# Softmax-weighted sums issued two key tiles at a time, with a third buffer of exponentials

## What is computed

```python
def _spatial_experts(xn, idx, in_w, in_b, out_w, out_b):      # S
    qkv = jnp.einsum('btd,bed->bte', xn, in_w[idx]) + in_b[idx][:, None, :]
    ...
    att = jax.nn.softmax(jnp.einsum('bthd,bshd->bhts', q, k), axis=-1)
    o = jnp.einsum('bhts,bshd->bthd', att, v).reshape(B, T, D)
...
    logits = jnp.where(causal, logits, -jnp.inf)               # T
    att = jax.nn.softmax(logits, axis=-1)
    o = jnp.einsum('bhts,bshd->bthd', att, v).reshape(B, T, D)
```

## Time and profile before

| | us |
|---|---|
| three runs, median (lowest to highest) | 1758.8 (1756.96 to 1760.89) |
| the profiled execution, its own time | 1757.12 |
| its span, first to last instruction | 1755.3 |
| TensorE busy | 1584.6 |
| VectorE busy | 1277.1 |
| ScalarE busy | 1117.8 |

### The profile page before, as it was taken

The page is one execution under the profiler, slowest core; times in us unless marked ns, Lnnn a source line. Parts: engine busy times, 40 slices in busy tenths (PEclk is TensorE's granted clock), DMA queues, the critical chain, the costliest instruction groups (busy, mean ns, idle before and its releaser), DMA issues. The chain is left out here.

```text
span 1755.3 us, 37109 instructions
## 1 busy us (share of the span) xinstructions
PE 1584.6 (90%) x9638; PEld 727.3 (41%) x9638; DVE 1277.1 (73%) x3087; ACT 1117.8 (64%) x2185; POOL 814.3 (46%) x865
## 2 busy tenths in 40 slices
PE   3668956999999999999999999999999999865998
PEld 1217942334434344434444343444444443211675
DVE  6886857388787887878787887879788787452442
ACT  3324850747777778687777778777777878714333
POOL 7832443345545545545544544544554553222443
PEclk9858966989999999999999999999999999956999
DMA  1211125366446546546546545645645644020221
GB/s 51 72 48 33 47 59 75 45 81 80 66 61 81 71 55 86 71 54 78 74 59 72 81 61 71 79 58 67 82 64 61 88 58 56 1 37 26 61 66 54
DMA packets 132339, 109.25 MB, mean 62 GB/s; under 512 B 21825, under 2 KB 125249, under 8 KB 132289
## 3 DMA queue, kind: packets, MB, share of 16 engines
q1 hardware_dynamic: 130240, 104.44, 42.0%
q0 software_dynamic: 2048, 4.20, 0.9%
HBM read 19.26 MB, written 8.39 MB: 16 GB/s over the span
## 5 line engine op out<-in xcount | busy, mean ns | idle before, releaser
L1032 ACT ACTIVATE probs<-psum 128x512 f32<-128x512 f32 (+3 forms) x1536 | 738.9, 552 | 316.7 <-PE psum L1137 197.7
L924 DVE TENSOR_REDUCE mx_S<-psum 128x1 f32<-128x512 f32 x512 | 323.3, 684 | 51.5 <-PE psum L1122 49.7
L924 DVE TENSOR_REDUCE mx_C<-psum 128x1 f32<-128x512 f32 x512 | 317.6, 681 | 46.7 <-PE psum L1122 45.4
L924 DVE TENSOR_REDUCE mx_T<-psum 128x1 f32<-128x128 f32 (+3 forms) x512 | 243.5, 489 | 120.8 <-PE psum L1125 108.1
L852 POOL CAST parts_q<-f_q 128x512 bf16<-128x512 f32 x48 | 29.2, 609 | 439.5 <-ACT f_q L1023 439.5
L1122 PE MATMUL psum<-ks_C,qs_C 96*128 96x512 bf16 x512 | 202.9, 398 | 5.1 <-DMA ks_C<-parts_k 1.0
L1122 PE MATMUL psum<-ks_S,qs_S 96*128 96x512 bf16 x512 | 199.8, 396 | 6.4 <-DVE mx_S L924 5.2
L1137 PE MATMUL psum<-qs_C,ks_C 99*128 99x512 bf16 x512 | 194.4, 391 | 10.6 <-DMA qs_C<-ng_p 6.4
L1137 PE MATMUL psum<-qs_S,ks_S 99*128 99x512 bf16 x512 | 195.9, 384 | 1.4 <-DMA qs_S<-ng_p 0.7
L1137 PE MATMUL psum<-qs_T,ks_T 99*128 99x256 bf16 (+3 forms) x512 | 153.2, 302 | 7.0 <-ACT probs L1032 5.6
L1122 PE MATMUL psum<-ks_T,qs_T 96*128 96x128 bf16 (+3 forms) x512 | 157.1, 309 | 1.2 <-DVE mx_T L924 0.9
(11 more groups left out here) (188 smaller groups left out, 2722.3 us busy)
## 6 DMA issues: line engine op xcount, KB each, us to landing
qs_S<-parts_q SPq DMA_DIRECT2D x96, 128.0 KB, 4.4
ks_S<-parts_k SPq DMA_DIRECT2D x96, 128.0 KB, 6.8
qs_T<-parts_q SPq DMA_DIRECT2D x96, 128.0 KB, 4.4
ks_T<-parts_k SPq DMA_DIRECT2D x96, 128.0 KB, 6.6
qs_C<-parts_q SPq DMA_DIRECT2D x96, 128.0 KB, 4.4
ks_C<-parts_k SPq DMA_DIRECT2D x96, 128.0 KB, 6.7
w_in_S<-in_s_in SPq DMA_DIRECT2D x16, 257.0 KB, 2.7
w_in_T<-in_t_in SPq DMA_DIRECT2D x16, 257.0 KB, 2.7
```

The source lines that it names most:

```text
L924: nc.vector.tensor_reduce(mx[kind][:, n:n + 1], psum[:, ring_place(kind, b, n, RL), 0:last_key], AX_X, ALU.max)\
L1032: nc.scalar.activation(probs[:, n // 4 % 2, n % 4, t0:T], psum[:, LOGITS + ring_place(kind, b, n, RC), t0:T], ACT.Exp, scale=SCALE).then_i ...
```

## The change

`weigh` is no longer called every fourth step, but twice in a row every eighth step: at step 3 for q = 4 and 5, at step 11 for q = 6 and 7, at step 19 for q = 0 and 1, at step 27 for q = 2 and 3. The groups with an even q so come four steps later than before; those with an odd q stay. `probs` gets a third buffer, and a group's first exponential waits for the group three before it. `s_outs` is laid into the third buffer of `probs`, which is unused at that time.

```diff
-RL, RC = 3, 3
+RL, RC, RP = 3, 3, 3
...
+def group_place(kind, b, q):
+
+    return ring_place(kind, b, 4 * q, 4 * RP) // 4
...
-        s_outs = sb("s_outs", [P, K, OUT_COLS])
...
-        probs = sb("probs2", [P, 2, 4, T])
+        probs = sb("probs2", [P, RP, 4, T])
+        s_outs = probs[:, RP - 1, 0:K, 0:OUT_COLS]
...
-                        at_least(act, summed, 8 * u + n // 4 - 1)
-                    nc.scalar.activation(probs[:, n // 4 % 2, n % 4, t0:T], psum[:, LOGITS + ring_place(kind, b, n, RC), t0:T], ACT.Exp,
+                        at_least(act, summed, 8 * u + n // 4 - RP + 1)
+                    nc.scalar.activation(probs[:, group_place(kind, b, n // 4), n % 4, t0:T], psum[:, LOGITS + ring_place(kind, b, n, RC), t0:T], ACT.Exp,
...
-                                                probs[:, q % 2, j, t0:T], start=(s == 0),
+                                                probs[:, group_place(kind, b, q), j, t0:T], start=(s == 0),
...
-                        if n % 4 == WEIGH_AT:
-                            q = (n - LAG) // 4 - 1
-                            if q < 0 and exists(bo):
-                                weigh(ko, bo, q + 8)
-                            if q >= 0 and exists(bb):
-                                weigh(kb, bb, q)
+                        if n % 8 == WEIGH_AT:
+                            q = 2 * ((n - LAG) // 8 - 1)
+                            for both in (q, q + 1):
+                                if q < 0 and exists(bo):
+                                    weigh(ko, bo, both + 8)
+                                if q >= 0 and exists(bb):
+                                    weigh(kb, bb, both)
```

More of the change, by code:

```diff
@@ L824, in _ @@
                     sp.dma_start(tile[:], source).then_inc(w_fixed, 16)
-                sp.dma_start(s_outs[:], s_out.rearrange("k p n -> p k n")).then_inc(s_outs_in, 16)
+                sp.dma_start(s_outs, s_out.rearrange("k p n -> p k n")).then_inc(s_outs_in, 16)
                 stack("S", 0)
```

## The result

| | before | after |
|---|---|---|
| median of the runs, us | 1758.9 (1756.96 to 1760.89) | 1824.0 (1822.86 to 1824.37) |
| profiled execution, span, us | 1755.3 | 1822.5 |
| one turn of the loop, us | 78.28 | 82.56 |
| ratio of after to before | | 1.037, 95% interval 1.036 to 1.038 |

The account below looks back on a forecast made before the run. TensorE, busy 90% of the span, bounds the kernel, closely coupled to VectorE and ScalarE. Windows gain 0.6 and lose 4.0 us, +3.4 a turn; over 15 turns 51 us, forecast 1810. Range 1778 to 1848, about 83%.

Parts of the forecast that it names:

- The chains: Time VectorE or ScalarE needs per eight-step window: 6.01 and 5.55 us plus extras; the longest, TensorE's included, sets the window.
- S slot, step 12: Eight-step window from step 12: VectorE's chain with the values ahead of the fifth maximum, 6.7 against 6.32 us, +0.4.
- Step 20: Windows from step 20: ScalarE's chain with the reciprocal, +0.9 us in S and T; C slot 5.0 against 5.24, -0.2.
- C slot, step 12: Eight-step window from step 12: VectorE's chain with the values, 6.5 against 5.76 us, +0.7.
- The four windows in bold: S slot from steps 12 and 20, T from 20, C from 12: together 2.9 us lost a turn.
- The pair: Two weighted sums in a row on TensorE: 2.00 us against 2.18, the second costing 0.91; 0.18 saved a pair.
- The windows from step 28: Last maxima and negation, next slot's projection: S 8.0 against 7.54 us, T 8.4 against 8.06, C 7.3 against 7.47.
- the T slot from step 4: Window where TensorE waits for ScalarE's copy of the second projection: 7.2 against 6.98 us, +0.2.
- (1) TensorE alone decides: Rival: VectorE and ScalarE lag too little to matter, the pairs save 35 us, 1724; 7%.
- (2) Cancelling: Rival: gain and loss cancel, time within 3.5 us of 1759; 4%.
- (3) The joint costs as much as a switch: Rival: the joint inside a pair saves nothing and the losses stand, 1848 us; 10%.
- (4) The clock: Rival: TensorE's granted clock falls from 1.00 to 0.88 through longer idle times, near 1890 us; 3%.

Follow-up runs that it names:

- the short reciprocal: Reciprocal's logarithm and exponential computed for 8 of 512 columns, in the kernel before (1748.7 us) and in the changed kernel (1798.2 us).
- pairs_narrow_only: Changed kernel with sums back at every fourth step, except T's two narrow couples, still issued in pairs; 1760.7 us, ratio 1.0012 to before.
- half maxima, half exponentials and a short reciprocal: Maxima and exponentials over half of each tile, reciprocal for 8 of 512 columns: 1695.7 us in the kernel before, 1688.2 in the changed one.
- short_recip_pairs: Changed kernel with the reciprocal's logarithm and exponential computed for 8 of 512 columns; 1798.2 us.

## Why the prediction was right

**The mechanism and the place** held. Lost time stands in the windows named, TensorE's waits for exponentials are 41.3 us in the whole span instead of 10.2, and the granted clock stays at 1.00 in each window. The next score comes 2.18 us after the last logits in the window shown, forecast 2.2. The runs show both halves of it: with VectorE and ScalarE made cheap, the pairs win. One reading of the earlier trace rows was too coarse: VectorE and ScalarE are not both busy for 5 to 6 us of each window, but for 3.87 to 6.49 and 3.58 to 5.77.

**The chains** were the steps that came out best. S slot, step 12: forecast 6.7, measured 6.72. Step 20: 6.8 and 6.80 in S, 6.7 and 6.69 in T. C slot, step 12: 6.5 and 6.49; step 20: 5.0 and 5.05. The four windows in bold lose 2.84 us a turn, against 2.9. Rounding helped: the terms for the S slot's step 20 add up to 6.84, not 6.8; the measured 6.80 is shorter by about the 0.05 by which the pair was taken too long. The logic of step 20 in the S slot (the sum at step 23 lay under ScalarE's chain, and comes out from under it) is confirmed by the short reciprocal, which takes 0.81 off that window and 0.17 off the same window of before (5.94 to 5.77): the loss there is 0.86 with the long reciprocal and 0.22 with the short one.

**The pair** was mis-sized a little: I took 0.91 for the second sum between ends of 0.86 and 1.09, and it is 0.86. In the trace the second half of the first sum starts 0.45 after the first half, and each half behind it 0.43 after the last; I had counted two halves of 0.46. The right price would have made the forecast up to 0.6 a turn shorter, and so further from the measured time.

**The size** was 3.4 us a turn and is 4.28. The windows from step 28 hold most of what is missing: forecast 8.0, 8.4 and 7.3, measured 8.15, 8.58 and 7.52, 0.55 in all. In the S slot the step that failed is "the projection of step 3 waits for the first of these to free its bank". It does not wait at all there; the transpose of step 1 does, 0.7 us, for the residual that frees the same bank (the wait, then the transpose and the projection):

```profile
PE psum L1195 <- DVE t_outT L994: 0.7, 1, 0.7
```

```profile
861.50 0.28 PE L1195 MATMUL psum<-ident,mx_S 128*32 128x128 f32 x1 [0.72 <-DVE t_outT L994]
...
862.56 1.07 PE L1110 MATMUL psum<-oT_S,w_fold 128*128 128x512 f32 x2
```

VectorE's negation in the same window:

```profile
861.89 0.27 DVE L936 TENSOR_SCALAR ng<-psum 32x128 f32<-32x128 f32 x1
```

The prediction does not name the transpose's wait. The negation came earlier than forecast, 4.40 us into the window and not 4.6; the projection starts at 5.07, where I had 4.9, because the transpose is late. In the T slot there are both waits, 0.5 for the residual and 0.4 for the negation; only the first is new, the second was 0.34 before. In the C slot the projection waits 0.48 for the negation in both kernels. Without the sum of step 31 it starts 4.66 us into the window instead of 5.46, and from there to the next window it is 2.86 instead of 2.01, since the sum now stands in the pair: the window gained nothing, where I had put 0.2. Another 0.16 is in the T slot from step 4 (7.36, not 7.2), where TensorE waits 0.4 for ScalarE's copy of the second projection: the wait was named, its size too small. What is left is under 0.1 in each window.

**The turns**: 13 in the loop give 13 x 4.28 = 55.6 us; the span grew by 67.2, so that the slots around the loop count as 2.7 turns, if all the rest is put down to them. I counted 2, though the 48 slots make 3. 15.7 x 4.28 = 67.2, against 15 x 3.4 = 51.

**The range** was in part luck. Its upper end, 1848, came from a pair that saves nothing, and the pair saved all that it could; no row stood behind the 1830 up to which my own forecast reached. What filled the room between 1810 and 1824 were the waits at steps 28 and 4 and the slots around the loop, which the range had not been made for.

**Windows as units.** Adding windows up worked since most begin with VectorE and ScalarE idle once there are pairs (VectorE at the start of ten of the twelve, ScalarE of all twelve). It does not hold one by one: the gain in the C slot from step 20 was the price of the window before it, as `pairs_narrow_only` showed.

**The rivals.** (1) TensorE alone decides: no; it takes half maxima, half exponentials and a short reciprocal for the pairs to gain, and then they gain 7.5 us. (2) Cancelling: no. (3) The joint costs as much as a switch: no, 0.86. (4) The clock: 1.00 in all twelve windows, with TensorE busy as little as 5.59 of 6.69 us. The rule of the Trainium skill on idle times between groups of matmuls ("TensorE: Matmul & The Clock Gate", section "A second HAM failure mode: psum-queue depth-cycling") tells of a kernel in which they made the clock swing. Here TensorE's waits in the windows from step 20 are 1.0 and 1.1 us long, and no window of this trace shows a swing; from 400 to 1500 us the granted clock is 1.00.

## What to carry to other kernels

Work on the bound engine that lets the other engines catch up is not overhead alone: before gathering it into longer pieces to save a switch, compare the longest stretch without a pause with what the buffers between the engines hold. Here a switch costs 0.23 us, but eight steps at 0.44 on TensorE against 0.60 on VectorE overrun three banks. One more buffer elsewhere (the third one of exponentials) does not help by itself if the short ones (scores and logits, three banks each) stay. And a sum that stands beside the other engine's long operation is almost free where it is, and costs its full time when it is moved behind it: the two windows with the reciprocal grew by 0.86 and 0.85 us, the price of the second sum of a pair.

## What the runs showed of the hardware

A group of eight float32 matmuls of 512 columns, 32 output rows each, holds TensorE for 0.86 us when it follows another such group, and for 1.00 us plus 0.09 ahead of it between bfloat16 matmuls. I had not expected the saving to be the whole fixed part. Nor that activations of 8 columns would still take time on the chain. In `short_recip_pairs`:

```profile
919.59 0.60 ACT L1038 ACTIVATE probs<-psum 128x512 f32<-128x512 f32 x1 [1.95 <-PE psum L1144]
920.09 0.20 ACT L1052 ACTIVATE s_log<-s_right 128x8 f32<-128x8 f32 x1
920.41 0.21 ACT L1055 ACTIVATE s_recip<-s_log 128x8 f32<-128x8 f32 x1
920.54 3.54 ACT L1038 ACTIVATE probs<-psum 128x512 f32<-128x512 f32 x7
```

From the first exponential to the second it is 0.95 us instead of 1.77 with 512 columns, and 0.48 with no reciprocal between them: two activations of 8 columns cost 0.47 us here, over a third of the 1.29 of the full ones. The window from step 20 of the T slot falls by as much as this distance does, from 6.69 to 5.88.
